# Six of eight output products moved into the recurrence, norms and fused products by halves, attention's norm batch by batch

## The reference, cut to what matters

```python
# mixer, one direction: D_INNER = 512 channels, D_STATE = 32 states, xr = x reversed for the second
u, z = split(x @ Win.T); uc = silu(conv4(u) + convb)
x_dbl = uc @ Wx.T                                # step sizes (rank 16), B (32), C (32)
dt = softplus(x_dbl[..., :16] @ Wdt.T + bdt)
h = exp(dt_t * A) * h + (dt_t * u_t) * B_t       # for each token t, channel and state
y_t = sum over states of h * C_t
out_d = layernorm(((y + uc * Dp) * silu(z)) @ Wout.T)
x = x + concat(out_forward, out_backward) @ Wfuse.T + bfuse
# cross-attention, 16 heads of 16, 361 keys for each sequence
x = x + softmax(q k / 4) v @ Wo.T + bo           # q from layernorm(x)
# experts: top 2 of 8 by a softmax of logits, and a shared one with weight 0.1, on layernorm(x)
x = x + sum of 2 routed experts + 0.1 * shared
```

## Time and profile before

| | us |
|---|---|
| median of 3 runs | 1123.24 (1118.74 to 1123.26) |
| the profiled execution | 1122.69 |
| its span, first to last instruction | 1120.8 |
| TensorE busy in the span | 1000.5 (89%) |
| VectorE, ScalarE, GpSimd busy | 806.4, 749.5, 626.9 |
| mean granted TensorE clock | 0.954 of full speed |

### The profile page before, as it was taken

How to read it: one execution, slowest core, us unless ns; L and a number is a source line. 1 busy time by engine, 2 the same in 40 slices (tenths; PEclk the granted TensorE clock), 3 DMA queues, 4 the chain that set the end, 5 groups by cost and what they waited for, 6 DMA issues and landing times.

```text
span 1120.8 us, 16809 instructions
## 1 busy us (share of the span) xinstructions
PE 1000.5 (89%) x5808; PEld 685.6 (61%) x5808; DVE 806.4 (72%) x954; ACT 749.5 (67%) x1725; POOL 626.9 (56%) x389
## 2 busy tenths in 40 slices
PE   5993998989989898998989898898989798999995
PEld 3542555546555565555555576676767564899995
DVE  6798999999999999999999836576657611211110
ACT  3999999999989899998988422556556431233331
POOL 2002999999999999999999804411110005022122
PEclk9995899999999999999999998899989799899998
DMA  5001334444444434434444303500000008689994
GB/s 187 8 7 56 102 112 112 112 111 111 111 112 112 112 111 112 112 112 112 111 112 109 69 1 113 158 26 29 1 1 2 1 1 309 186 267 328 302 309 116
DMA packets 91118, 125.44 MB, mean 112 GB/s; under 512 B 11641, under 2 KB 84490, under 8 KB 91018
## 3 DMA queue, kind: packets, MB, share of 16 engines
q1 hardware_dynamic: 87130, 120.04, 37.7%
q0 software_dynamic: 3904, 4.33, 2.0%
HBM read 115.93 MB, written 9.23 MB: 112 GB/s over the span
## 4 chain that ended last, share of the span: by engine, by line
PE 39%; DVE 30%; issue 12%; DMA 10%; ACT 7%; another core or an unknown queue 1%; DVEq 0%; POOLq 0%; ACTq 0%
DVE states L1718 19%; PE ps L1210 10%; DMA sums<-y_tile,x_tile 10%; PE ps L1088 5%; DVE states L1696 5%; PE ps L1098 4%; PE ps L1190 3%; PE ps L1316 2%; PE ps L1328 2%; DVE neg_max L1800 2%; PE ps L1464 2%; PE ps L1105 2%; ACT probs L1010 2%; PE ps L1473 2%; PE ps L1527 1%
## 5 line engine op out<-in xcount | busy, mean ns | idle before, releaser
L685 POOL TENSOR_TENSOR states<-states,c_row 128x800 f32<-128x800 f32 x255 | 473.7, 1934 | 90.2 <-DVE states L1718 90.2
L1210 PE MATMUL ps<-states,ident 128*128 128x400 f32 x1024 | 375.2, 509 | 11.4 <-DVE u L1726 11.4
L1210 PEld LDWEIGHTS ps<-states,ident 128*128 128x128 f32 x1024 | 187.3, 193 | 127.6 <-DVE u L1726 12.7
L1718 DVE TENSOR_TENSOR_SCAN states<-sb_decay,ps 128x800 f32<-128x800 f32 x128 | 231.2, 1807 | 5.0 <-ACT sb_decay L924 3.8
L1718 DVE TENSOR_TENSOR_SCAN states<-ps,states 128x800 f32<-128x800 f32 x128 | 229.7, 1795 | 1.1 <-ACT ps L924 1.1
L916 ACT ACTIVATE xT<-xn_tok,xT 100x256 f32<-100x256 f32 x512 | 216.5, 493 | 1.1 <-PE ps L1190 0.9
L924 ACT ACTIVATE ps<-dt,neg_a 128x396 f32<-128x396 f32 x256 | 141.2, 583 | 46.5 <-DVE states L1718 46.0
L1190 PEld LDWEIGHTS ps<-ident,xT 100*128 100x128 f32 x1024 | 97.6, 145 | 104.1 <-issue 87.8
L1190 PE MATMUL ps<-ident,xT 100*128 100x100 f32 x1024 | 115.1, 257 | 43.9 <-DVE states L1718 30.9
L924 ACT ACTIVATE sb_decay<-dt,neg_a 128x396 f32<-128x396 f32 x256 | 144.4, 611 | 1.0 <-DVE states L1718 0.9
L1010 ACT ACTIVATE probs<-ps,neg_max 100x361 f32<-100x361 f32 x128 | 70.9, 560 | 64.5 <-DVE neg_max L1800 63.9
(11 more groups left out here) (225 smaller groups left out, 1252.8 us busy)
## 6 DMA issues: line engine op xcount, KB each, us to landing
c_row<-rows SPq DMA_DIRECT2D x256, 200.0 KB, 3.1
w_tile<-in_w SPq DMA_DIRECT2D x40, 1024.0 KB, 5.1
b_row<-rows SPq DMA_DIRECT2D x32, 200.0 KB, 3.1
ctx<-in_ctxT SPq DMA_DIRECT2D x8, 361.0 KB, 4.3
rows_by_slot<-blank_rows SPq DMA_DIRECT2D x1, 2660.0 KB, 11.7
x_tile<-rows_by_slot SPq DMA_DIRECT2D x20, 133.0 KB, 3.8
win<-in_winT SPq DMA_DIRECT2D x2, 1024.0 KB, 10.3
w_shared<-in_w SPq DMA_DIRECT2D x2, 1024.0 KB, 6.6
```

Source lines behind the costliest of these rows:

```text
L685: nc.gpsimd.tensor_tensor(st, st, c_row[i % C_SLOTS][:].unsqueeze(1).broadcast_to([P, CP, TQ]), ALU.mult).then_inc(product_ready, 1)
L1210: mm = nc.tensor.matmul(ps[:, j, 0:TQ], ident[:], states[i % RING][:, j * TQ:(j + 1) * TQ], start=(n == 0), stop=(n == N - 1), skip_group_ ...
L1718: nc.vector.tensor_tensor_scan(st, rates, inflows, 0.0, ALU.mult, ALU.add).then_inc(scan_done, 1)
```

## The change

Six of the eight mixing products (`MIX_EARLY`) are made inside the recurrence, one for each of segments 2 to 7. A product's eight matmuls stand at steps 18, 20, ... 32 of the segment, each ahead of that iteration's `sum_state`, in bank 7. ScalarE copies the result at step 3 of the next segment; it goes into storage of `dt_sb` and `dtu` that is no longer read. Bank 7 also holds the turned `dtu`, so the two wait for each other. The last state is multiplied with C whole by VectorE.

Behind the recurrence the statistics of the first direction are taken before the last gate; VectorE then norms eight sequences of the first direction at once, four of the second, and, after some copies, the last four. The first fused product comes before the last turning.

In attention the statistics and moments of sequence b-1 are taken in groups 3 and 4 of b. In the last sequence ScalarE takes the root for seven at group 6, ahead of its copy, VectorE applies four norms there and three behind the last group, and the eighth is normed alone. The first half is turned before the last heads are projected, the second after two units of the shared expert. VectorE copies that second half. The logits follow unit 2 and the ranks unit 6; the exponential of the logits is at unit 2 in place of 3. Some tiles lie elsewhere in memory.

```diff
-LOGITS_AT, RANKS_AT, ROWS_AT = 1, 8, 13
+SECOND_HALF_AT, LOGITS_AT, RANKS_AT, ROWS_AT = 1, 2, 6, 13
+STATS_AT, MOMENTS_AT, ROOT_AT = 3, 4, H // 2 - 2
+MIX_EARLY = ((0, 0), (0, 1), (0, 2), (0, 3), (1, 0), (1, 1))
+MIX_FROM, MIX_AT, COPY_MIX_AT = 2, (18, 20, 22, 24, 26, 28, 30, 32), 3
+MIX_BANK, MIX_NORMS = 7, 3
...
+            def copy_mix(j):
+                act.wait_ge(mix_done, j + 1)
+                d, h = MIX_EARLY[j]
+                nc.scalar.activation(mix_pair[d][h], pairs_of(ps[0:L, MIX_BANK, :]), ACT.Copy).then_inc(mix_copied, 1)
...
+                if s > MIX_FROM and n == COPY_MIX_AT:
+                    copy_mix(s - 1 - MIX_FROM)
...
+            copy_mix(len(MIX_EARLY) - 1)
+            root(Q + 1, 0, B)
+            root(Q + 2, B)
+            for h in range(B // 4, B // 2):
+                copy_out(("mix", 1, h), mix_pair[1][h], pairs_of(bank(("mix", 1, h))[0:L, :]))
...
+                    if (b, g) == (B - 1, ROOT_AT):
+                        root(2 * Q + MIX_NORMS + 1, 0, B - 1)
                     copy_probs(b, g)
...
-                    if i == STEPS - 1:
-                        pe.wait_ge((product_ready, last_half)[j], (STEPS, 1)[j])
+                else:
+                    pe.wait_ge(last_product, 1)
...
+            def mix_early(j, part):
+                d, h = MIX_EARLY[j]
+                s = j + MIX_FROM
+                b, c = 2 * h + part // CT, part % CT
+                if part == 0:
+                    pe.wait_ge(dtu_tok_ready, 2 * min(s + 2, SEG))
+                    if j:
+                        pe.wait_ge(mix_copied, j)
+                mm = nc.tensor.matmul(ps[0:L, MIX_BANK, part // CT * D:(part // CT + 1) * D],
+                                      u_sb[d][:, c, b * L:(b + 1) * L], wout_sb[d][:, c, :], start=(c == 0),
+                                      stop=(c == CT - 1), skip_group_check=True)
+                if part == len(MIX_AT) - 1:
+                    mm.then_inc(mix_done, 1)
...
+                for at in MIX_AT:
+                    j = (i - at) // N - MIX_FROM
+                    if (i - at) % N == 0 and 0 <= j < len(MIX_EARLY):
+                        mix_early(j, MIX_AT.index(at))
                 behind = i - SUM_LAG
...
+            turn_mixed(0, 0)
+            turn_mixed(1, 0)
+            turn_mixed(0, 1)
+            fuse(0)
+            turn_mixed(1, 1)
+            for h in range(1, B // 2):
+                fuse(h)
...
-            project_heads(B - 1)
...
+            turn_x3(0)
+            project_heads(B - 1)
...
+                if u == SECOND_HALF_AT:
+                    turn_x3(1)
...
-            st = states[last % RING][:, TQ:W]
-            nc.vector.tensor_tensor(st, st, c_row[last % C_SLOTS][:], ALU.mult).then_inc(last_half, 1)
+            st = states[last % RING][:].rearrange("p (c t) -> p c t", c=CP)
+            nc.vector.tensor_tensor(st, st, c_row[last % C_SLOTS][:].unsqueeze(1).broadcast_to([P, CP, TQ]), ALU.mult
+                                    ).then_inc(last_product, 1)
...
+            dve.wait_ge(mix_copied, B // 2)
+            all_stats(0, mix_tok[0])
             gated(SEG - 1)
+            all_moments(0, B)
+            dve.wait_ge(mix_copied, len(MIX_EARLY))
+            all_stats(B, mix_tok[1][0:BQ])
+            all_applied(0, mix_tok[0])
+            all_moments(B, BQ)
+            all_applied(B, mix_tok[1][0:BQ])
...
+                    if b > 0 and g == STATS_AT:
+                        dve.wait_ge(x2_ready, b)
+                        norm_stats(b - 1, x_tok[:, b - 1, :])
+                        steps += 1
+                    if b > 0 and g == MOMENTS_AT:
+                        dve.wait_ge(dve_step, steps)
+                        norm_moments(b - 1)
+                        steps += 1
...
+                    if (b, g) == (B - 1, ROOT_AT):
+                        norm_root(0, B - 1)
+                        for j in range(BQ):
+                            norm_apply(j, x_tok[:, j, :], rows_src[:, j, 0:D])
...
+            for j in range(BQ, B - 1):
+                norm_apply(j, x_tok[:, j, :], rows_src[:, j, 0:D])
             copy_heads(B - 1)
             normalise_heads(B - 1)
-            norm_x(0, rows_src)
             add_attention(B - 1)
             dve.wait_ge(x2_ready, B)
-            norm_x(1, rows_src)
+            layer_norm(B - 1, [(x_tok[:, B - 1, :], rows_src[:, B - 1, 0:D])])
+            for k in range(KD):
+                copy_out(("xn3T", k, 1), xn3T[:, k, chunk(1)], bank(("xn3T", k, 1))[:, 0:TQ])
```

More of the change, by code:

```diff
@@ L169, in bank_jobs, with turns @@
         for h in range(B // 2):
-            jobs.append((("mix", d, h), "a"))
-    for q in range(Q):
-        for d in range(DIRS):
-            for k in range(KD):
-                jobs.append((("mixT", d, k, q), "v" if k else "a"))
-    for h in range(B // 2):
+            if (d, h) not in MIX_EARLY:
+                jobs.append((("mix", d, h), "a"))
+    def turns(d, q):
+        for k in range(KD):
+            jobs.append((("mixT", d, k, q), "v" if k else "a"))
+    turns(0, 0)
+    turns(1, 0)
+    turns(0, 1)
+    jobs.append((("fuse", 0), "v"))
+    turns(1, 1)
+    for h in range(1, B // 2):
         jobs.append((("fuse", h), "v"))
@@ L274, in decoder_layer @@
         late = ExitStack()
[L275 removed]
+        mix_pair = [[(dt_sb, dtu)[h // 2][d][0:L, 2 * (h % 2):2 * (h % 2) + 2, 0:D] for h in range(B // 2)]
+                    for d in range(DIRS)]
+        mix_tok = [[mix_pair[d][b // 2][:, b % 2, :] for b in range(B)] for d in range(DIRS)]
         attn = ExitStack()
@@ L979, in copy_mixed @@
                          scale=lng_sb[:, j:j + 1], bias=lnb_sb[:, j:j + 1])
-            for q in range(Q):
-                for d in range(DIRS):
-                    copy_mixed(d, 0, q)
+            copy_mixed(0, 0, 0)
+            copy_mixed(1, 0, 0)
+            copy_mixed(0, 0, 1)
+            root(Q + MIX_NORMS, B + BQ)
+            copy_mixed(1, 0, 1)
             def high_queries(m, q):
@@ L1582, in layer_norm, with norm_root @@
+            def norm_root(at, size):
                 nonlocal norms
                 norms += 1
-                cols = slice(at, at + BQ)
-                for j, (src, _) in enumerate(pairs):
-                    later(nc.vector.bn_stats(stats[:, at + j, :], src))
-                dve.wait_ge(dve_step, steps)
-                for j in range(BQ):
-                    later(nc.vector.bn_aggr(moments[:, at + j, :], stats[:, at + j, :]))
-                dve.wait_ge(dve_step, steps)
-                nc.vector.tensor_scalar(var_eps[:, cols], moments[:, cols, 1], EPS, None, ALU.add
-                                        ).then_inc(moments_ready, 1)
+                cols = slice(at, at + size)
@@ L1593, in layer_norm, with norm_apply @@
                 dve.wait_ge(std_ready, norms)
                 step(nc.vector.reciprocal(rstd[:, cols], std[:, cols]))
+            def norm_apply(at, src, dst):
+                nc.vector.tensor_scalar(dst, src, moments[:, at, 0:1], rstd[:, at:at + 1],
+                                        ALU.subtract, ALU.mult).then_inc(xn_ready, 1)
+            def layer_norm(at, pairs):
+                nonlocal steps
+                for j, (src, _) in enumerate(pairs):
+                    norm_stats(at + j, src)
+                steps += len(pairs)
+                dve.wait_ge(dve_step, steps)
+                for j in range(len(pairs)):
+                    norm_moments(at + j)
+                steps += len(pairs)
+                dve.wait_ge(dve_step, steps)
+                norm_variance(at, len(pairs))
+                norm_root(at, len(pairs))
@@ new lines, in _, with all_stats, all_moments @@
+            nc.vector.tensor_tensor(st, st, c_row[last % C_SLOTS][:].unsqueeze(1).broadcast_to([P, CP, TQ]), ALU.mult
+                                    ).then_inc(last_product, 1)
+            def all_stats(at, src):
+                nonlocal steps
+                for j, t in enumerate(src):
+                    norm_stats(at + j, t)
+                steps += len(src)
+            def all_moments(at, size):
+                nonlocal steps
+                dve.wait_ge(dve_step, steps)
+                for j in range(size):
+                    norm_moments(at + j)
+                steps += size
+                dve.wait_ge(dve_step, steps)
+                norm_variance(at, size)
```

133 lines of the change are left out of this document (71 added, 62 removed).

## The result

The changed kernel takes 1088.10 us, median of 4 runs (1087.61 to 1089.18), beside 1122.13 (1118.74 to 1123.26, 4 runs) of the kernel before on the same chip: ratio 0.971, 95% interval 0.9693 to 0.9726. The profiled execution took 1087.61, its span 1085.5, against 1120.8.

The account below looks back on a forecast made before the run. VectorE was taken to bound the recurrence, TensorE the later stages. -23.1 to the end of the fused products, +1.2 for their clock and -4.5 after attention gave -26.4 from 1122.7: forecast 1096.5, range 1090 to 1105.

Parts of the forecast that it names:

- Ranks two units earlier and logits one later give nothing: Shared expert after attention: the reordering was priced at nothing, its matmuls taken to run back to back.
- a fetch stall moves. Gone: 1089: Rival: ScalarE's stall while experts' weights stream, costing 7.7 us, disappears, giving 1089; chance 8%.
- The mixing part: Recurrence to the end of the fused products: mixing products moved early and norms rearranged, gain 21.9 us.
- the worked-out 25.1 us (646.2 to 671.3): After the last gate: mixing products start at 646.2 and the fused products end at 671.3, before it was 694.4.
- The 1.2 us added for a drop of the clock: Fused products: the new gap ahead may lower TensorE's clock, bounds 0 and 2.5 us, taken as +1.2.
- 1.2 in slips: Recurrence: VectorE loses about 0.2 us to late TensorE once in each of six segments, +1.2.
- 1.0 in the tail: Last segment: products at iterations 254 and 256 cost 0.9, plus 0.1 of lateness, +1.0.
- the spare time: Recurrence: TensorE needs 14.3 us for eight steps against VectorE's 16.4, so 2.1 us spare; early products take 1.74.
- The last product by VectorE: End of recurrence: VectorE's whole product with C is ready two us before the sum needs it, gain nothing.
- 0.5 more than the half without cover: End of recurrence: without TensorE's cover, VectorE's whole product with C would cost 0.5 us more than the half.
- Behind attention: Attention's end to third shared unit and logits: -3.1 at lower clock, -10.1 at full clock, -4.5 taken.
- the 2.7 forecast: End of attention: TensorE idles 2.7 us ahead of its last turning, where it idled 1.25, +1.5.

Follow-up runs that it names:

- act_shifted: The kernel before with 16 small copies added on ScalarE behind shared units 4 to 7: 1122.48 us, ratio 0.9995 to before.
- mix_only: The changed kernel with attention's norm, the order behind attention, logits and ranks as before: 1097.54 us, ratio 0.9783 to before.
- early_twice: The changed kernel with each of the 48 early matmuls of the mixing products issued twice: 1104.34 us, ratio 0.9866 to before.
- root_later: The changed kernel with ScalarE's root in attention's last batch behind its copy of group 6, VectorE's scaling behind the last group: 1085.92 us, ratio 0.9706 to before.
- scatters_split: The kernel before with GpSimd waiting for ScalarE's two cwT copies after 8 of its 16 scatters: 1120.28 us, ratio 0.9993 to before.
- scatters_held: The kernel before with GpSimd waiting for ScalarE's two cwT copies before its first scatter: 1130.82 us, ratio 1.009 to before.
- before_again: The kernel before once more, unchanged: 1121.58 us, one run.
- last_halves: The changed kernel with the last product with C again by halves, one by GpSimd and one by VectorE: 1093.38 us, one run.

## Why the prediction came out too high

**The step that failed** is "Ranks two units earlier and logits one later give nothing: the matmuls of the shared expert run back to back". They don't run back to back: the earlier trace rows has TensorE idle 4.97 us in the middle and at half clock behind it, and the prediction priced just this as a rival of 7.7 us. What it lacked was the link. The ranks set when the scatters start, the scatters set when ScalarE gets on, 22.8 us later, and TensorE wants hidden unit 14 a fixed number of units behind the ranks: in the kernel before at 950.99 - 4.97 = 946.0, or 18.5 us after the first scatter, 5 us too early; in the changed kernel at 918.08 - 0.22 = 917.9, or 23.9 after it. Two units of 2.69 us are these 5.4, and they are what hides the stall. The rival "a fetch stall moves. Gone: 1089" had the right time at a chance of 8%, with a cause that act_shifted speaks against. In the rows TensorE's wait shrank by 4.75 us and the eight matmuls behind it by 2.49, 7.2 in all; with them the sum would have been 1089.3.

**The mixing part** was forecast at -21.9 and measured at -25.2 by the medians (mix_only against before). From the first scan to the last exponentials of attention it is -21.7 in the profile of mix_only and -23.0 in that of the changed kernel. Mechanism and size are right. From the gate to the end of the fused products the worked-out 25.1 us (646.2 to 671.3) came out as 25.06. The 1.2 us added for a drop of the clock wasn't there (1.00 in that window): TensorE waited 0.30 and 0.61 us, where 1 us and more were expected.

**The recurrence** was forecast to lose 1.2 in slips and 1.0 in the tail. The tail, from last scan to gate, grew by 0.9 (8.49 to 9.35). Up to the last scan the changed kernel lost 0.7 and mix_only, with the same recurrence, 1.4, so together 1.6 and 2.3 against 2.2. The slips aren't as even as forecast: segments take 66.6 or 67.3 us where they took 66.5 or 66.9. early_twice shows that the spare time was counted rightly.

**The last product by VectorE**, nothing: 9.36 and 9.35 us. That the whole product would cost 0.5 more than the half without cover was wrong: 2.80 us against 3.39.

**Behind attention** -4.5 was taken between -3.1 at the lower clock and -10.1 at the full one. It is -5.7 in the table, and about -4.3 once the drop behind the logits is counted on the same side in both kernels; a choice between two bounds so far apart came this near partly by luck. The upper bound was too far by 1.4: it halves the logits at full clock, and they take 2.91 us at 1.00. TensorE's wait of 2.65 us ahead of the last turning is the 2.7 forecast, and root_later shortens it by 1.5.

**The experts** stayed, 161.5 and 161.6. Row by row the span was missed by 8.9 us: 5.5 in the shared expert, 1.2 each at the start and behind attention, 1.1 between gate and attention, 0.6 in the recurrence, less 0.7 in attention and the experts.

## What to carry to other kernels

An idle time in a trace whose cause isn't known still has a position and an end: ask what it starts with and what it ends with, and check whether a reordered step shifts one against the other, before pricing the step at nothing. Work can be moved into an engine's spare time as long as the sum over a period leaves a little; here 0.44 us in every two steps was nearly free and twice that cost 2.2 us a segment. A gain on one side of a join is kept only if the other side, here the rows behind the scatters, isn't late next. Where the clock drops in one of two executions of the same program, a boundary between stages that falls beside the drop moves 1.5 us from one row of a table to the next.

## What the runs showed of the hardware

- 16 indirect DMAs in a row on GpSimd, 1.30 us apart, stop ScalarE from 11 to 17 us after the first until 22.7 to 22.9 us after it, though they share no data and no semaphore with it; an instruction or two can get through on the way. The first eight of scatters_split didn't. Direct loads at 367 GB/s (scatters_held, 926 to 936) didn't.
- Filling TensorE's idle time with matmuls kept the granted clock at 1.00, against 0.65 from 856 to 862 and 0.78 from 862 to 868 in root_later without it.
- 32 matmul records of 8 columns took 2.91 us at a clock of 1.00. The unit behind them ran at the lower level in 12 of the 16 traces; it didn't in before_again, mix_only, scatters_held and root_later. What decides it isn't shown.
- A product of VectorE with two inputs next to GpSimd's ended 0.43 us after the last of GpSimd's for 400 columns (before: 639.90 and 639.47; last_halves: 641.58 and 641.15) and 0.85 us after it for 800 (after: 638.65 and 637.80).
